# Attention over a sorted graph: one gather in sixteen replaced by a one-hot matmul

## The reference

```python
edge_index = jnp.stack([src, dst])
x = _layernorm(x + _L0_gnn_ref(x, edge_attr3_2x64, src, dst), axis=-1)
x = _layernorm(x + _L1_gnn_ref(x, Wq, Wk, Wv, Wout, edge_index), axis=-1)
# L0: q = 0.95 * max(z)[src] * e1 + e0;  z_new = 0.2 z + 0.8 segsum(q, dst) / segsum(e1, dst)
# L1, with 4 heads:
s = jnp.einsum('hef,hef->eh', Q[:, receiver], K[:, sender]) * scale
m = jax.ops.segment_max(s, receiver, num_segments=n)
p = jnp.exp(s - m[receiver])
alpha = p / segment_sum(p, receiver)[receiver]
out = mean over heads of segment_sum(alpha * V[:, sender], receiver)
return x + out @ Wout
```

## Time and profile before

| | us |
|---|---|
| timed runs, median of 3 (2589.87 to 2590.60) | 2590.28 |
| the profiled execution's own time, given by its span (first to last instruction) | 2997.5 |
| first gather to last gather in it | 526.7 to 2906.6 |

### The profile page before, as it was taken

The page is one execution under the profiler, slowest core; times in us unless marked ns, Lnnn a source line. Parts: engine busy times, 40 slices in busy tenths (PEclk is TensorE's granted clock), DMA queues, the critical chain, the costliest instruction groups (busy, mean ns, idle before and its releaser), DMA issues.

```text
span 2997.5 us, 65526 instructions
## 1 busy us (share of the span) xinstructions
PE 2424.3 (81%) x18960; PEld 1749.1 (58%) x18961; DVE 1716.4 (57%) x5572; ACT 1313.2 (44%) x3792; POOL 1892.7 (63%) x2370
## 2 busy tenths in 40 slices
PE   4999998477888888887878788888888877778877
PEld 3888887254655555555555555555555555555555
DVE  8999997454545454444444444454544444444447
ACT  5555553443444344443444344443444343434434
POOL 3888887464666666666566566666666555656640
PEclk9999995665555555555555555555555555655558
DMA  6887772111111111111121111211112111112101
GB/s 177 257 255 254 254 252 51 21 31 33 32 38 32 39 38 33 38 32 37 30 38 31 36 35 36 38 32 39 37 33 39 29 36 30 37 29 39 31 18 24
DMA packets 178767, 194.85 MB, mean 65 GB/s; under 512 B 98339, under 2 KB 101235, under 8 KB 176481
## 3 DMA queue, kind: packets, MB, share of 16 engines
q1 hardware_dynamic: 128294, 138.91, 16.5%
q0 software_dynamic: 50048, 51.35, 9.1%
HBM read 184.87 MB, written 5.25 MB: 63 GB/s over the span
## 4 chain that ended last, share of the span: by engine, by line
another core or an unknown queue 30%; DVE 29%; issue 21%; DVEq 10%; PE 7%; ACT 1%; POOL 1%; ACTq 0%; DMA 0%; POOLq 0%; SPq 0%
DVE O L886 5%; DVE rmax L955 5%; DVE nm_old L968 4%; DVE l_st L883 3%; DVEq L982 2%; DVE big L723 2%; DVE cur L971 2%; DVEq L908 2%; DVE XT L877 1%; DVE nm_st L974 1%; DVEq L746 1%; DVEq L886 1%; PE psS L1513 1%; DVEq L904 1%
## 5 line engine op out<-in xcount | busy, mean ns | idle before, releaser
L589 POOL DMA_INDIRECT XS<-x_dram,dst_bs x1564 | 1482.4, 948 | 900.6 <-issue 419.9
L883 DVE SCALAR_TENSOR_TENSOR l_st<-l_st,alpha,rsum 64x1 f32 x782 | 168.2, 215 | 925.0 <-remote 891.3
L1471 PE MATMUL psVX<-XS,PmPT 128*128 128x64 f32 x1568 | 334.4, 385 | 243.6 <-ACT PmPT L1237 243.6
L1513 PE MATMUL psS<-XT,Ubuf 96*128 96x512 f32 x522 | 505.8, 1071 | 17.5 <-issue 6.2
L1471 PEld LDWEIGHTS psVX<-XS,PmPT 128*128 128x128 f32 x1568 | 308.8, 293 | 302.5 <-ACT PmPT L1237 302.2
L1237 ACT COPY PmPT<-psT 128x512 f32<-128x512 f32 x196 | 114.7, 585 | 760.1 <-remote 727.8
L1471 PE MATMUL psM<-XS,dst_bs 128*128 128x64 f32 x1560 | 343.2, 398 | 60.6 <-ACT dst_bs L1237 49.4
L1471 PEld LDWEIGHTS psM<-XS,dst_bs 128*128 128x128 f32 x1560 | 341.6, 321 | 71.0 <-ACT dst_bs L1237 58.3
L955 DVE TENSOR_REDUCE rmax<-psS 128x1 f32<-128x512 f32 x391 | 270.2, 691 | 34.2 <-remote 12.7
L1513 PE MATMUL psS<-dst_bs,Ubuf 96*128 96x512 f32 x260 | 250.3, 1065 | 7.1 <-ACT Ubuf L1188 1.6
L1466 PE MATMUL psT<-ident,dst_bs 128*128 128x128 f32 x780 | 207.6, 419 | 37.1 <-issue 34.2
(11 more groups left out here) (281 smaller groups left out, 4133.2 us busy)
## 6 DMA issues: line engine op xcount, KB each, us to landing
big<-in_edge_attr_2x SPq DMA_DIRECT2D x342, 256.0 KB, 3.3
big<-dst_turned SPq DMA_DIRECT2D x49, 512.0 KB
XS<-x_dram,dst_bs POOLq DMA_INDIRECT x1564
O<-in_edge_attr_2x SPq DMA_DIRECT2D x48, 256.0 KB, 3.4
O<-codes_dram SPq DMA_DIRECT2D x200, 6.0 KB
x_dram<-x SPq DMA_DIRECT2D x12, 128.0 KB, 1.9
out<-big SPq DMA_DIRECT2D x12, 128.0 KB
codes_dram<-O SPq DMA_DIRECT2D x3, 384.0 KB
```

The source lines that it names most:

```text
L589: pool.indirect_dma_start(xs(k, j), None, x1_dram, bass.IndirectOffsetOnAxis(ap=idx2[b % SB][:, k * CPP + j:k * CPP + j + 1], axis=0)).the ...
L883: dve.scalar_tensor_tensor(out=ls, in0=ls, scalar=al[half], in1=rs[half], op0=ALU.mult, op1=ALU.add)
L1471: last = pe.matmul(ps, pt[:, j * P:(j + 1) * P], xs(J % S2, j), start=(j == 0), stop=(j == CPP - 1))
L1513: pe.matmul(psSc[1 - a][:, :], Ubuf[1 - a][:, :], XT[(J - 1) % 3][:, :], start=True, stop=True).then_inc(s_done, 1)
```

## The change

One gather of every fourth chunk, the fourth gather of chunks 12, 16, ..., 388, is computed on the chip. The 128 wanted rows of a chunk r * 4 are a selection out of 6272 rows of x1. A node's block number b is split as b = 7 s + l, into a group s and a lane l of 7 each. For every such chunk a code `s * 128 + p` of each wanted node is broadcast to all partitions. VectorE compares it with the partition's seven codes, which gives seven one-hot matrices of 128 x 128 (`look_hot`). TensorE multiplies each with the 7 lanes x 64 features of its group, for each of three bf16 parts of x1 (`look`, 7 x 3 matmuls into `psL`, 448 columns, which is in the bank `psA`). VectorE keeps of the seven lanes the one that is wanted and adds up over the lanes (`look_pick`: one `scalar_tensor_tensor` and one `tensor_reduce`), straight into the chunk's slot.

The three bf16 parts take 1.5 times the room of x1, so x1 in SBUF shares its buffer with them and the splitting overwrites it, group by group, in steps 1 to 6 and just after (`part_of`, on VectorE and ScalarE). x1 is loaded back from `x1_dram` after the last look, and the centring that VectorE did in steps 3 to 6 is done by GpSimd then, with means taken before the splitting. The codes are made in step 0, stored to DRAM and loaded row by row by SP. The scratch in SBUF for GpSimd's DMA descriptors is halved.

`mean_and_codes` is a reduce of 49 blocks of 64 and six short steps on 101 x 128 integers; `look_pick` stands inside `attend`, after the update, when J % 4 == 1.

```diff
+    LE = 4
+    LG = 7
+    LW = LG * D
+    LR0 = 3
...
+        tab_x1 = sb("tab_x1", [P, NB * D // 2 + NB * D])
+        parts = tab_x1[:, :].bitcast(BF16).rearrange("p (s k c) -> p s k c", s=LG, k=3)
+        x1 = tab_x1[:, NB * D // 2:]
...
+            sp.wait_ge(s_lcode, 1)
+            sp.dma_start(code_dram, code_row[:, :]).then_inc(s_lcst, 16)
+            sp.wait_ge(s_lcst, 16)
+            sp.wait_ge(s_up, UG)
...
             def block(b, i):
                 more = 0 if i is None else i
                 sp.wait_ge(upd, S2 * (b - SB + 1) + more * (2 * SB * S2))
                 load_ids_of(b, more)
                 load_dst_of(b, more)
+                for r in (2 * b, 2 * b + 1):
+                    sp.wait_ge(l_hot, r - 1 - LR0 + more * LPI)
+                    load_code(r, more)
...
+            sp.wait_ge(l_sum, LEND + 1 - LR0)
+            sp.dma_start(x1v[:, :, :], x1_dram.rearrange("(b p) d -> p b d", p=P)).then_inc(s_x1b, 16)
...
-                for j in range(CPP):
+                for j in range(CPP - 1 if c % LE == 0 and c // LE >= LR0 else CPP):
                     if j == CPP // 2 and c >= S2:
                         pool.wait_ge(s_done, c - S2 + 6)
                     pool.indirect_dma_start(xs(k, j), None, x1_dram, ...
+            pool.wait_ge(s_x1b, 16)
+            for g in range(TG):
+                pool.tensor_tensor(x_, x_, x1_mean[:, b0:b0 + nb].unsqueeze(2).broadcast_to([P, nb, D]), ALU.add).then_inc(s_x1c, 1)
             for g in range(TG):
                 ...
                 pool.memset(aggT[g % 2], 0.0).then_inc(s_zero_agg, 1)
...
+            def part_of(k):
+                if k > 0:
+                    dve.wait_ge(s_tmid, k)
+                    dve.tensor_tensor(parts[:, k - 1, 2, :], hot_pick[:, :], parts[:, k - 1, 1, :], ALU.subtract).then_inc(s_tlo, 1)
+                    dve.wait_ge(s_tlo, k)
+                if k < LG:
+                    dve.wait_ge(s_thi, k + 1)
+                    dve.tensor_tensor(hot_pick[:, :], x1[:, k * LW:(k + 1) * LW], parts[:, k, 0, :], ALU.subtract).then_inc(s_trest, 1)
+
+            def look_hot(J, i):
+                r = (J + LE + 1) // LE
+                q = r % 2
+                dve.wait_ge(l_code[q], 16 * ((r - 1) // 2) + i * (8 * LPI))
+                dve.wait_ge(looked, r - LR0 + 1 + i * LPI)
+                dve.tensor_tensor(hot.rearrange("p (s e) -> p s e", s=LG), code_b[q].unsqueeze(1).broadcast_to([P, LG, P]),
+                                  code_of.unsqueeze(2).broadcast_to([P, LG, P]), ALU.is_equal).then_inc(l_hot, 1)
+
+            def look_pick(J, i):
+                r = (J + 3) // LE
+                dve.wait_ge(l_sum, r - LR0 + 1 + i * LPI)
+                dve.scalar_tensor_tensor(out=hot_pick[:, :], in0=lane_of, scalar=lane_col[:, bass.ds(i * LPI + r, 1)], in1=psL,
+                                         op0=ALU.is_equal, op1=ALU.mult).then_inc(l_pick, 1)
+                dve.wait_ge(l_pick, r - LR0 + 2 + i * LPI)
+                dve.tensor_reduce(xs(r * LE % S2, CPP - 1), hot_pick[:, :].rearrange("p (l f) -> p f l", f=D), AX_X, ALU.add).then_inc(looked, 1)
...
             for m in range(H2):
                 attend(m, m, None)
+                if m == 0:
+                    mean_and_codes()
+                if m == 1:
+                    keep_lanes()
                 if m == 2:
                     centre_weights()
-                    dve.wait_ge(s_x1d, 16 * UG)
-                for g in range(TG):
-                    if m > 2 and g % 4 == m - 3:
-                        centre_x1(g)
+                if m > 0:
+                    part_of(m - 1)
...
                 for k in range(U2):
                     attend(i * U2 + (H2 + k), H2 + k, i)
+                    if k % LE == 0:
+                        look_hot(H2 + k, i)
...
+            def part_of(k):
+                if k > 0:
+                    act.wait_ge(s_trest, k)
+                    act.copy(parts[:, k - 1, 1, :], hot_pick[:, :]).then_inc(s_tmid, 1)
+                if k < LG:
+                    act.copy(parts[:, k, 0, :], x1[:, k * LW:(k + 1) * LW]).then_inc(s_thi, 1)
...
+                    if i is not None and J % LE == 0:
+                        pe.wait_ge(looked, J // LE - LR0 + 2 + i * LPI)
...
+            def look(J, i):
+                pe.wait_ge(s_tlo, LG)
+                pe.wait_ge(x_upd, pe.snap(xv, min_val=1))
+                pe.wait_ge(l_hot, (J + LE) // LE - LR0 + 1 + i * LPI)
+                for t in range(LG):
+                    for k in range(3):
+                        last = pe.matmul(psL, hot[:, t * P:(t + 1) * P], parts[:, t, k, :], start=(t == 0 and k == 0), stop=(t == LG - 1 and k == 2))
+                last.then_inc(l_sum, 1)
...
                 for k in range(U2):
                     attend(i * U2 + (H2 + k), H2 + k, i)
+                    if k % LE == 1:
+                        look(H2 + k, i)
...
-    nc = bacc.Bacc("TRN2", target_bir_lowering=False, num_devices=1)
+    nc = bacc.Bacc("TRN2", target_bir_lowering=False, num_devices=1, dynamic_dma_scratch_size=8192)
```

More of the change, by code:

```diff
@@ L69, in gnn_resnorm_kernel @@
     assert U2 == 2 * SB * S2 and H2 < S2
+    LEND = (NCH + 1) // LE
+    LROWS = LEND + 2
+    LPI = U2 // LE
+    TM = TP_ // 16 * 16
+    assert NB == LG * LG and U2 % LE == 0 and S2 == 2 * LE and H2 == LE + 3 and LR0 * LE == H2 + 5 and (NCH + 1) % LE == 0 and LEND == TP_ and NCH % LE == 3 and (LEND - 1) * LE * CH + CH <= E
     ctx = ExitStack()
@@ L105, in gnn_resnorm_kernel @@
         assert t1 + 2 * RE <= ta and 3 * RE <= SB1 * SC and NB * D <= 2 * RE
-        x1 = sb("x1", [P, NB * D])
+        tab_x1 = sb("tab_x1", [P, NB * D // 2 + NB * D])
+        parts = tab_x1[:, :].bitcast(BF16).rearrange("p (s k c) -> p s k c", s=LG, k=3)
+        x1 = tab_x1[:, NB * D // 2:]
+        look_ids = tab_x1[0:LROWS, 0:CH].bitcast(I32)
+        hot_pick = sb("hot_pick", [P, LW])
+        hot = hot_pick[:, :].bitcast(BF16)
+        look_hi, look_s = (hot_pick[0:LROWS, k * P:(k + 1) * P].bitcast(I32) for k in range(2))
+        lane_row = hot_pick[0:LROWS, 2 * P:3 * P]
+        lane_col = sb("lane_col", [P, LROWS])
+        code_row = sb("code_row", [LROWS, P])
         x1v = x1[:, :].rearrange("p (b d) -> p b d", d=D)
@@ L150, in gnn_resnorm_kernel @@
         assert SB * S2 * CH <= ta and SB * S2 * CPP <= CH
+        f0 = 3 * CH + SB * S2 * CPP
+        lane_of = dst_bs[:, f0:f0 + LW // 2].bitcast(BF16)
+        code_of = dst_bs[:, f0 + LW // 2:f0 + LW // 2 + LG].bitcast(F32)
+        assert f0 + LW // 2 + LG <= 4 * CH and LG * P == 2 * LW
+        code_b = [A[:, 2 * q:2 * q + 2, :].rearrange("p h d -> p (h d)") for q in range(2)]
+        x1_mean = stat[:, 3 * NB:4 * NB]
         dst_perm = big[0:TP_, t1 + RE:t1 + 2 * RE]
@@ L248, in gnn_resnorm_kernel @@
         turn_steps = sem("turn_steps")
+        s_lids, s_lcode, s_ltr, s_lcst, s_liota, s_thi, s_trest, s_tmid, s_tlo, s_x1b, s_x1c = (
+            sem(n) for n in ("look_ids_loaded", "look_codes_made", "look_lanes_turned", "look_codes_stored", "look_iotas",
+                             "table_hi", "table_rest", "table_mid", "table_lo", "x1_back", "x1_centred"))
+        l_code = [sem(f"look_code_loaded{q}") for q in range(2)]
+        l_hot, l_sum, l_pick, looked = (sem(n) for n in ("look_hot", "look_sum", "look_picked", "looked"))
+        psL = psA[:, 0:LW]
         ld2 = [sem(f"dst2_loaded{k}") for k in range(SB)]
@@ L420, in load_chunks @@
                 load_dst_of(b, 0)
+            sp.wait_ge(s_const, 8)
+            sp.dma_start(look_ids[0:TM, :], src[0:TM * RE].rearrange("(r e) -> r e", e=RE)[:, 0:CH]).then_inc(s_lids, 16)
+            for r in range(TM, LEND):
+                sp.dma_start(look_ids[r:r + 1, :].rearrange("a (k e) -> a k e", k=16),
+                             src[r * RE:r * RE + CH].rearrange("(a k e) -> a k e", a=1, k=16)).then_inc(s_lids, 16)
             sp.wait_ge(s_dstt, 1)
@@ L433, in _, with load_code @@
                 sp.dma_start(x1_dram[b0 * P:(b0 + nb) * P, :].rearrange("(b p) d -> p b d", p=P), x1v[:, b0:b0 + nb, :]).then_inc(s_x1d, 16)
+            def load_code(r, more):
+                row = code_dram[r:r + 1, :] if isinstance(more, int) else code_dram[bass.ds(more * LPI + r, 1), :]
+                sp.dma_start(code_b[r % 2], row.broadcast_to([P, P])).then_inc(l_code[r % 2], 16)
+            sp.wait_ge(s_lcode, 1)
+            sp.dma_start(code_dram, code_row[:, :]).then_inc(s_lcst, 16)
+            sp.wait_ge(s_lcst, 16)
+            sp.wait_ge(s_up, UG)
+            for r in range(LR0, 2 * SB):
+                if r - 2 >= LR0:
+                    sp.wait_ge(l_hot, r - 1 - LR0)
+                load_code(r, 0)
             def block(b, i):
@@ L486, in _ @@
             pool.wait_ge(s_const, 7)
+            pool.memset(look_ids[TM:LROWS, :], 0).then_inc(s_const, 1)
+            pool.wait_ge(s_const, 8)
             pool.memset(ones[:, :], 1.0)
@@ L963, in attend @@
```

(8 more changed lines are left out.)

52 lines of the change are left out of this document (43 added, 9 removed).

## The result

The changed kernel took **2650.34 us** (median of 4 runs, 2646.17 to 2659.54) against 2590.07 us for the kernel before in the same comparison: 1.0241 of its time, 95% interval 1.0218 to 1.0263. It is slower by 60 us; 2503 was forecast, and the sign was the unlikelier one (0.30). The range holds the time by luck: its stretch up to 2700 was there for rival 1, a clock that stays low, and that is not what happened.

What follows compares the result with a forecast made beforehand. GpSimd's gather issue was taken as the bound, 20.0 us per four chunks. 2590.3 - 118.8 (gathers) + 19 (port) + 6 (start) + 3 (end) + 3 (second visits) gave 2503 us, range 2473 to 2700.

Steps and rivals of the forecast that it cites:

- the sign: Whether the whole kernel gets faster or slower: faster 0.64, same 0.06, slower 0.30.
- rival 1: Attention loop: TensorE's clock mostly stays at 1.2 GHz, loop 21.8 to 23.1 us, 2770 to 2895 us; 0.29 with Rival 4.
- The bound and the late releases: Attention: GpSimd's gather issue sets 20.0 us per four chunks; 399 us of late waits belong to the profiled execution only.
- Rival 4: Attention: late releases also occur in timed runs, so gathers save nothing and time is as in rival 1; 0.29 together.
- The look: TensorE's 21 added matmuls per four chunks: 4.1 us at 2.4 GHz, 8.0 at 1.2 GHz, taken as 4.1 to 6.
- The loop of four chunks: Attention: VectorE's 15.7 us plus 2.3 us of waits give 18.0 us at 2.4 GHz, under GpSimd's 18.75.
- rival 2: Attention loop: clock drops now and then, loop 19.2 to 19.9 us, 2525 to 2585 us; chance 0.15.
- the last term: Attention: chunks needing a second visit have longer steps that find less slack, adding 3 us.
- The port: GpSimd gathers beside VectorE's hot: 0.2 us lost per look, 96 looks, +19 us, bounds 0 to 45.
- rival 3: Attention: hot blocks GpSimd for its whole 1.1 us, +106 us, total 2590, no change; 0.06 with other even outcomes.
- The start: Before and in the first steps: means, codes and splitting of x1 add 6 us, from 2 to 12.
- The end: After the last look: x1's reload and 13 additions are hidden; last look and TensorE's lag add 3 us, 0 to 10.

Runs made afterwards that it cites:

- filler: Changed kernel plus six matmuls of 448 bf16 columns, product unused, where TensorE waits for exp in steps with J % 4 = 2: 2585.26 us, 0.998.

## Why the prediction was wrong, by its steps

- **The bound and the late releases** were right: 115 us for 95 gathers, and a span of 2588.0 in a second profile. Rival 4 falls with them.
- **The look** was right: 4.14 us (4.1 forecast) at 2.4 GHz. It took longer where it began at 1.2 GHz (mean of 96: 4.33). Hot was right too, 1.09. Reduce was not: 0.91 us for 448 elements where the line through the reduces of 64 and 256 in the earlier trace rows gave 0.62; pick took 0.68.
- **The loop of four chunks**, forecast at 18.0 us, takes 18.04 where TensorE holds 2.4 GHz (27 of 85), so VectorE's own time plus its waits was the right sum, though reduce was undersized. The 1.6 us of pick and reduce stand in a series with the look: 2.33 to 2.78 us VectorE for TensorE, then 1.76 TensorE for VectorE. What the sum left out is the clock: it took 2.4 GHz for every loop, while in 58 of 85 the clock falls behind those waits, and the mean is 19.40. Taking out pick and reduce (-109), filling the idle time (-65) and shortening the look (-102) each show a link of it; they overlap and may not be added, since GpSimd's 18.75 us are the floor. Between the two kernels without visits the loop costs 68 - 16 = 52 us of waiting, by the mechanism that rival 2 described (clock drops now and then, 19.2 to 19.9 us, 2525 to 2585; 2514 without visits).
- **The step that failed is the last term**, "I add 3 us for the chunks that need a second visit, whose longer steps now find less slack", together with the loop that it hangs on. The 11 visits cost 17.5 us before and 136 after, 119 more and not 3, and that is what turns the sign. GpSimd's issue needed 20.0 us for four chunks where the other engines were done sooner, and a visit of some 10 us was made up for by the chunks behind it. Loops of 19.4 us over 18.75 have nothing to make it up with. The 3 us had no working behind them: even a loop of 18.0 leaves 0.75 us for four chunks, some 7 us between two visits on average (an estimate, 391 chunks and 11 visits). With the shorter look and filler together, visits in place, GpSimd has one wait of over 3 us left where the changed kernel has 15, so the visits' price is not their own but the loop's. The parts come to what was measured: 2590.3 - 118.8 + 52 in the loop + 8 at start and end + 119 for the visits is 2650.5. Each is a difference of two runs and good to some 10 us (the kernel without visits ran from 2505 to 2534).
- **Rival 1**, the clock, took the right side for a reason half right. The clock does fall in most loops, but for about one step: the granted clock from 600 to 2400 us was 0.84, not 0.56, and 70 of the 294 steps without a look took 4.3 to 4.9 us, not two or three of four. The 0.56 belonged to the execution with late releases; the second profile of the kernel before has 0.67 in its attention stretch. The point from which rival 1 was to decide, 20.0 us, is passed only with visits (2014.3 us for 1468 intervals, 20.6 us for four chunks). By the rule of the Trainium skill (TensorE: Matmul & The Clock Gate, Part 4) that transposes don't count as activity, the clock should have fallen behind each look. It held through the step right behind the look, and in 27 of 85 loops through all steps. Where it fell, it fell after idle time, and with filler in this idle time it held in 71 of 85. So the runs tie the fall here to waiting in part; the same waiting did not bring it every time, and that transposes weigh less is neither shown nor excluded.
- **The port** (19 us, rival 3 at 106) was sized right, and still it is not part of the price. 140 gathers overlap with hot; together they take 19.0 us more than 0.944 us each. The 23 gathers of over 1.25 us all overlap with hot, and the longest takes 1.515. But GpSimd waits elsewhere anyway, and leaving hot out gave nothing back. By the Trainium skill (SBUF — State Buffer, Who interferes with whom) the second instruction is blocked in full, which would be up to 105 us here. The trace agrees in part: the longest gathers began 0.40 us into hot and took 0.57 us more than usual, where 0.69 us of hot were left; but hot took at most 1.15 us, also in the 86 cases where a gather had begun before it.
- **The start** shows little: the first gather goes out between 526.4 and 530.3 us in the changed kernel and its variants, between 526.3 and 527.7 in the kernel before and its own (6 us forecast). The 27 us of idle time at the 33rd gather in the earlier trace rows were also of that one execution: here it follows in 1.25 us. **The end** (from the last gather on) cost 14 us against the kernel with the gathers alone left out, and 10 between the two kernels without visits, not 3. x1's return is hidden, as forecast; what shows is that the other engines are further behind when the last gather goes out:

```profile
2544.57 0.95 POOL L649 DMA_INDIRECT XS<-x_dram,dst_bs  x1 [0.31 <-issue]
2574.52 7.35 POOL L657 TENSOR_TENSOR tab_x<-tab_x,stat 128x256 f32<-128x256 f32 x13 [29.00 <-DMA tab_x<-x_dram]
2592.11 0.56 POOL L663 MEMSET PmPT<- 128x256 f32 x2 [10.24 <-DVE O L1135]
```

GpSimd has added the means back by 2581.9 and waits 10.24 us more for VectorE. That the other engines are behind is read from this one wait; no run takes it away.

## What to carry to other kernels

Slack under the engine that sets the pace is not free to spend: it pays for rare long steps. Before an edit that moves work from the bound engine to the others, count the rare steps and what each would cost with the new slack; here 11 of 391 chunks turned -61 us into +60. A loop in which two engines wait for each other can have two lengths, one at each level of the clock: here 18.0 and 19.5 us, with the pace of 18.75 between them, so a sum at 2.4 GHz alone had the right number and the wrong answer. Where a trace of one execution has waits that the timed runs can't have, take a second profile before slack or idle time is read from it.

## What the runs showed of the hardware that was not expected

- Added matmuls made the kernel faster: 576 of them, 6 beside each look, took 65 us off, with the clock granted at 0.94 in place of 0.84.
- Idle time of 1.76 and 0.55 us on TensorE, in a step that had begun at 2.4 GHz, was followed by 1.2 GHz in 58 of 85 loops and not in the other 27. With 0.64 and 0.54 us of idle time behind filler 71 of 85 loops held 2.4 GHz throughout; with the same idle time and the filler one step earlier 52 of 84 did.
- A gather of GpSimd that began 0.40 us into a VectorE instruction of 1.09 us with two operands in SBUF took 1.51 us in place of 0.94; VectorE's instruction, begun during a gather, stayed at 1.09 to 1.15.
- A reduce from 448 elements to 64 sums of seven, each sum's elements 64 places apart, took 0.91 us; one of 512 in a row to one value, the row maximum, 0.69.
